# Layer 0's experts computed with units on partitions; layer 1 ranks keys in three pieces per tile; three copies moved to ScalarE; new order tables for both layers

## The reference

```python
x = L0_attn_x                                  # (8, 512, 256)
xn = layernorm(x)
x = x + gated_retention(xn) + experts(xn)      # layer 0
xn = layernorm(x)
x = x + state_space(xn) + mixed_attention(xn)  # layer 1

# experts: E=8, hidden 128, the two best of eight per token
scale = softmax(xf @ gate_w), zero but for each token's top 2
xs = scale.T[:, :, None] * xf[None]            # the INPUT is scaled, per expert
h  = silu(xs @ w1) * (xs @ w3)
out = (h @ w2).sum over experts
```

## Time and profile before

| | us |
|---|---|
| median of 3 runs | 2124.76 |
| lowest, highest | 2121.08, 2131.89 |
| the profiled execution | 2114.17 |
| its span, first to last instruction | 2112.4 |

### The profile page before, as it was taken

One profiled execution on the slowest core, in us unless ns is written; L12 is line 12 of the kernel. 1 busy time (PEld: TensorE's weight loads), 2 busy tenths in 40 slices (PEclk: granted clock), 3 DMA queues, 4 the chain that ended last, 5 costly groups with the idle time before them and its releaser, 6 DMA issues.

```text
span 2112.4 us, 44569 instructions
## 1 busy us (share of the span) xinstructions
PE 1967.1 (93%) x14499; PEld 1188.0 (56%) x14499; DVE 1676.8 (79%) x3065; ACT 1287.0 (61%) x2889; POOL 1396.8 (66%) x1053
## 2 busy tenths in 40 slices
PE   7999999999999977698999999999999998998898
PEld 4666666666666654454464564554554554654555
DVE  5777677677776743598888988989988989989997
ACT  4453534444353425468669779679678678678664
POOL 3433333435233320598888989989979979979996
PEclk9999999999999998699999999999999999999999
DMA  5111202021111116423534533633633533643621
GB/s 150 38 47 49 64 21 62 26 62 44 43 39 34 44 53 188 121 70 111 159 91 112 163 103 97 163 108 92 168 105 108 160 109 93 170 122 90 166 85 31
DMA packets 117427, 198.84 MB, mean 94 GB/s; under 512 B 27688, under 2 KB 64456, under 8 KB 117200
## 3 DMA queue, kind: packets, MB, share of 16 engines
q1 hardware_dynamic: 117200, 196.00, 33.6%
HBM read 148.94 MB, written 46.99 MB: 93 GB/s over the span
## 4 chain that ended last, share of the span: by engine, by line
PE 36%; POOL 11%; issue 7%; DVE 7%; ACT 1%; POOLq 0%; DMA 0%; DVEq 0%; SPq 0%; ACTq 0%
PE bank L1776 32%; POOL HB L1721 7%; POOL HB L1727 4%; PE bank L1876 2%; DVE HB L2244 2%; DVE Sel L2232 1%; DVE bank L2244 1%; PE bank L1782 1%; POOL SD L1747 1%; PE bank L1796 1%; DVE Sel L2230 1%; DVE nmax L2268 0%; DVE HB L2249 0%; PE bank L1848 0%; POOL G L1731 0%
## 5 line engine op out<-in xcount | busy, mean ns | idle before, releaser
L1721 POOL TENSOR_TENSOR HB<-DD,BC 128x512 f32<-128x512 f32 x512 | 643.9, 1284 | 92.3 <-PE bank L1776 73.4
L2058 ACT ACTIVATE bank<-DD,A 128x512 f32<-128x512 f32 x512 | 349.4, 690 | 102.4 <-DVE HB L2249 74.9
L1727 POOL TENSOR_TENSOR HB<-HB,BC 128x512 f32<-128x512 f32 x256 | 331.0, 1304 | 40.9 <-DVE HB L2244 40.6
L2244 DVE TENSOR_TENSOR_SCAN bank<-bank,HB 128x512 f32<-128x512 f32 x256 | 312.0, 1219 | 33.8 <-POOL HB L1721 17.2
L2244 DVE TENSOR_TENSOR_SCAN HB<-bank,HB 128x512 f32<-128x512 f32 x256 | 310.6, 1213 | 13.6 <-ACT bank L2058 6.1
L444 POOL TENSOR_TENSOR hr<-hs,half 128x16 f32<-128x16 f32 x32 | 93.0, 2907 | 250.9 <-DVE hs L968 250.9
L469 PE MATMUL bank<-W,XT 128*128 128x512 f32 x512 | 242.7, 621 | 4.1 <-DVE KT L896 4.0
L2249 DVE TENSOR_TENSOR HB<-bank,BC 128x512 f32<-128x512 f32 x256 | 175.3, 685 | 13.4
L469 PEld LDWEIGHTS bank<-W,XT 128*128 128x128 f32 x512 | 98.9, 200 | 117.5 <-issue 116.3
L1776 PE MATMUL bank<-HB,fold 128*32 128x512 f32 x1024 | 137.2, 607 | 19.5 <-POOL HB L1727 12.3
L1999 ACT ACTIVATE PT<-bank 128x512 f32<-128x512 f32 x192 | 113.0, 594 | 61.4 <-PE bank L1876 61.2
(11 more groups left out here) (236 smaller groups left out, 4069.8 us busy)
## 6 DMA issues: line engine op xcount, KB each, us to landing
DD<-dd_scratch SPq DMA_DIRECT2D x512, 128.0 KB, 3.4
ROW<-row_scratch SPq DMA_DIRECT2D x64, 256.0 KB, 4.0
BC<-ssm_scratch SPq DMA_DIRECT2D x128, 128.0 KB, 4.7
US<-us_scratch SPq DMA_DIRECT2D x32, 512.0 KB, 4.5
us_scratch<-U SPq DMA_DIRECT2D x8, 1024.0 KB, 4.2
us_scratch<-SD SPq DMA_DIRECT2D x8, 1024.0 KB, 6.5
dd_scratch<-SD SPq DMA_DIRECT2D x8, 1024.0 KB, 4.2
dd_scratch<-U SPq DMA_DIRECT2D x8, 1024.0 KB, 6.5
```

Of the source, the lines that this page charges most:

```text
L1721: done(pool.tensor_tensor(HB[:, c % HR], du, bc, ALU.mult), "dbu")
L1727: done(pool.tensor_tensor(h, h, bc, ALU.mult), "cg")
L2058: done(act.activation(PD[n % 2][:], delta, ACT.Exp, scale=A[:, k:k + 1]), "dA")
L2244: done(dve.tensor_tensor_scan(h if n % 2 else dA, dA, h, 0.0, ALU.mult, ALU.add), "scan")
```

## The change

1. Layer 0's experts are turned: hidden units stand on partitions. The scales are transposed (`ct`, PE), copied to SBUF (`ctc`, ACT), stored to DRAM (`cst`, SP) and read back as a row that is broadcast to all partitions, one expert at a time (`cld`, SP, 3 buffers). POOL multiplies XT by that row (`xs`, 128x1024, 2 buffers). `up` has an expert's W1 or W3 as the stationary operand and streams XS, 512 tokens. SiLU and the product are one instruction each per expert (128x512), written to HT, which is already the operand that `dn` needs: `ht` and `htc` go. `wo` and all eight experts of a tile are summed in one PSUM bank, so that one `ya` per tile remains.
2. `dec`, `SQ`, `junk`, `prod` shrink to two buffers or fewer (SBUF space).
3. `rank` compares the keys of earlier tiles with >=, those of its own and later tiles with >, and tests ties in its own 128 only. `ranks` is two additions.
4. `xtv`, `stv` and the copy of the two heavy `widenc` (now `widenr`) go from DVE to ACT.
5. All the order tables have new numbers.

```diff
-L0_PERIOD = 260.34
+L0_PERIOD = 296.85
+                def scales_store(b):
+                    after(sp, "ctc", b, 0)
+                    if b >= 2:
+                        scales_read(sp, b - 2, E - 1)
+                    sp.dma_start(scr["sc"][b % 2].rearrange("(q p) -> q p", p=P), CT[0:NT * E]) \
+                      .then_inc(over["sc_st"], 16)
+
+                def scales_load(b, e):
+                    sp.wait_ge(over["sc_st"], 16 * (b + 1))
+                    n = E * b + e
+                    if n >= SCS:
+                        after(sp, "xs", *divmod(n - SCS, E))
+                    row = scr["sc"][b % 2, e * T:(e + 1) * T].unsqueeze(0).broadcast_to([P, T])
+                    sp.dma_start(SCB[:, n % SCS], row).then_inc(over[f"sc_in{n % SCS}"], 16)
+                def scaled_input(b, e):
+                    after(pool, "xta", b, 0)
+                    after(pool, "xtv", b, 0)
+                    row = scales_loaded(pool, b, e)
+                    after(pool, "up", *lag(b, e, 2, E))
+                    done(pool.tensor_tensor(XS[:, e % 2], XT[:, b % 2], mid(row, ND), ALU.mult), "xs")
+                def turn_scales(b):
+                    after(pe, "ew2", b, 0)
+                    bank = claimed(pe, "ct", b, 0)
+                    done(pe.transpose(bank[0:NT * E, 0:P], SC[:, b % 2].rearrange("p e t -> p (e t)"), ident[:]), "ct")
-                            q = mm(bank[:], xt[:, k, t * P:(t + 1) * P],
-                                   W[:, k, 4 * g:4 * g + 4].rearrange("p e h -> p (e h)"), k == 0, k == ND - 1)
+                            q = mm(bank[:], W[:, k, e], XS[:, e % 2, k], k == 0, k == ND - 1)
-                def turn_hidden(b, n):
...
+                def down(b, t):
+                    after(pe, "ogc", b, t)
+                    after(pe, "hd", b, *range(E))
...
+                    for k in range(ND):
+                        mm(bank[:, 0:D], OGT[:, k, rows], Wo[:, k], k == 0, False)
+                    for e in range(E):
+                        q = mm(bank[:, 0:D], HT[:, e, rows], W2[:, e], False, e == E - 1)
+                def hidden_silu(b, e):
+                    after(act, "up", b, e)
+                    after(act, "dn", b - 1, *range(NT))
+                    done(act.activation(HT[:, e], banks.of["up", b, 2 * e][:], ACT.Silu), "si")
+                def hidden(b, e):
+                    after(dve, "si", b, e)
+                    done(dve.tensor_tensor(HT[:, e], banks.of["up", b, 2 * e + 1][:], HT[:, e], ALU.mult), "hd")
...
-                    own(dve.tensor_scalar(KJ[:, 0], KR[:], KC[:, t:t + 1], None, ALU.is_gt, ALU.add,
-                                          accum_out=ahead[:, t:t + 1]))
-                    own(dve.scalar_tensor_tensor(out=KJ[:, 1], in0=KR[:], scalar=KC[:, t:t + 1],
-                                                 in1=before[:, (3 - t) * P:(3 - t) * P + T],
-                                                 op0=ALU.is_equal, op1=ALU.mult, accum_out=ties[:, t:t + 1]))
+                    own_tile = slice(t * P, (t + 1) * P)
+                    if t:
+                        own(dve.tensor_scalar(KJ[:, 0, 0:t * P], KR[:, 0:t * P], KC[:, t:t + 1], None, ALU.is_ge, ALU.add,
+                                              accum_out=ahead[:, 0, t:t + 1]))
+                    own(dve.tensor_scalar(KJ[:, 0, t * P:], KR[:, t * P:], KC[:, t:t + 1], None, ALU.is_gt, ALU.add,
+                                          accum_out=ahead[:, 1, t:t + 1]))
+                    own(dve.scalar_tensor_tensor(out=KJ[:, 1, 0:P], in0=KR[:, own_tile], scalar=KC[:, t:t + 1],
+                                                 in1=before[:], op0=ALU.is_equal, op1=ALU.mult,
+                                                 accum_out=ties[:, t:t + 1]))
```

More of the change, by code:

```diff
@@ new lines @@
+    "x_ld": [-875.81],
+    "bn": [-763.34, -789.48, -798.06, -824.33],
+    "agg": [-747.25],
+    "rs1": [-731.67],
+    "xn1": [-645.44, -668.0, -632.76, -682.52],
+    "xt": [-549.41, -546.41],
+    "xta": [-538.03],
+    "xtv": [-539.83],
+    "sm": [-528.01],
+    "smc": [-510.44],
+    "ga": [-500.78],
+    "gl": [-486.97],
+    "gm": [-497.17],
+    "gx": [-453.82],
+    "ew0": [-402.53],
+    "ew1": [-353.32],
+    "ew2": [-292.61],
+    "ct": [-278.03],
+    "ctc": [-277.28],
+    "cst": [-242.4],
@@ L297, in lag, with scales_read, scales_loaded @@
             return (b, t - n) if t >= n else (b - 1, t + count - n)
[L299 to L304, removed]
+        def scales_read(eng, b, e):
+            n = E * b + e
+            for m in range(max(n - SCS + 1, 0), n + 1):
+                eng.wait_ge(over[f"sc_in{m % SCS}"], 16 * (m // SCS + 1))
+        def scales_loaded(eng, b, e):
+            n = E * b + e
+            eng.wait_ge(over[f"sc_in{n % SCS}"], 16 * (n // SCS + 1))
+            return SCB[:, n % SCS]
         with nc.Block() as block:
@@ L793, in _ @@
                         hidden_silu(b, i)
[L794 to L795 removed]
+                    elif what == "ctc":
+                        scales_turned(b)
             @block.vector
@@ new lines @@
+    "ssm": [-86.102],
+    "ssmc": [-85.841],
+    "ssm_st": [-84.459],
+    "dt_ld": [-78.255],
+    "abs": [-61.875, -57.944, -74.582, -68.648],
+    "sexp": [-54.145],
+    "relu": [-70.772, -61.822, -36.311, -40.936],
+    "sln": [-49.381],
+    "del": [-43.372, -30.319],
+    "du": [-40.007, -30.297],
+    "dd_st": [-23.626],
+    "xrt": [-65.423, -59.553],
+    "xrtc": [-64.131, -55.098],
+    "k_ld": [-62.642],
+    "rank": [-29.71, -14.81, -6.725, -23.568],
+    "ranks": [3.121],
+    "sel": [13.514, 20.757, 17.944, 20.82],
@@ L2117, in _ @@
                         copied(XT[:, 0], "xt", b, 0, "xta")
+                    elif what == "xtv":
+                        after(act, "del", b - 1, 0)
+                        copied(XT[:, 1], "xt", b, 1, "xtv")
                     elif what == "xr":
@@ L2152, in _ @@
                         copied(SelT[:, 0], "st", b, 0, "sta")
+                    elif what == "stv":
+                        after(act, "tail", b - 1, *range(NT))
+                        copied(SelT[:, 1], "st", b, 1, "stv")
+                    elif what == "widenr":
+                        after(act, "widen", b, NT + i)
+                        after(act, "tail", b - 1, *range(NT))
+                        done(act.activation(YR[:, i], PB[6 + i % 2][:, 0:D], ACT.Copy), "widenr")
                     elif what == "turnc":
@@ L2306, in _ @@
                 number()
+                own(dve.memset(ahead[:, 0, 0:1], 0.0))
                 for what, b, i in plan:
@@ L2317, in _ @@
                         bound(b)
-                    elif what == "xtv":
-                        turned(b)
                     elif what == "conv":
@@ L2339, in _ @@
                         widened(b, i)
-                    elif what == "stv":
-                        selected(b)
                     elif what == "tailc":
```

764 lines of the change are left out of this document (349 added, 415 removed), and 175 rows, old and new, of tables (AT, FIRST, L0_AT, LAST).

## The result

The changed kernel takes 2066.7 us (median of 4 timed runs, 2061.9 to 2072.7) beside 2128.3 us (2121.1 to 2135.8) for the kernel before on the same chip: ratio 0.971, 95% interval 0.967 to 0.976, that is 51 to 71 us faster. The profiled execution took 2064.1 us, 50.1 less than that of before.

A forecast was written before the change was run, and what follows sets the result against it. PE was taken to bound layer 0, and PE, DVE and POOL in turns layer 1. Layer 0's -20 and layer 1's -14 make -34 us, from the timed 2124.8 to 2091 us; range 2056 to 2122.

The forecast's parts named there:

- PE bounds layer 0: Layer 0: PE, busy 669.5 of 679.0 us, sets the time, so work taken off it comes off the time.
- Transposes -28: Layer 0, PE: the 64 `ht` that go, at 0.44 us each, save 28 us.
- The lock's +4: Layer 0: DVE waits for POOL's `xs` at the shared SBUF ports; 4 us reach PE, bounds 0 to 27.
- The head's +3: Start of layer 0: `up` comes later, behind scales, transpose, DRAM round trip and `xs`; 3 us lost, bounds 0 to 8.
- Layer 0 together: Sum for layer 0: -28 + 1 + 4 + 3 = -20 us, bounds -30 to +10.
- The carried 10.6 us: Whole kernel: the old profiled execution, 2114.2 us, was 10.6 below the timed median, 2124.8; this difference was carried over.
- Layer 1: Layer 1: -2 us per period from DVE's relief and the new order, bounds -6 and +5; about -14 us over seven periods.
- The ranking: Layer 1, DVE: shorter tie tests against more comparisons and a second `ranks` addition, net -0.2 us per batch.
- A period 5 us shorter: Rival, layer 1: the new tables also shorten the period by 5 us, giving 2058 us; chance 0.22.
- Layer 1 gives nothing: Rival: PE and POOL keep their load in layer 1, so only layer 0's -20 remains, 2105 us; chance 0.13.
- The lock eats layer 0: Rival: DVE's state chain waits for `xs`, PE's idle time grows by 20; layer 0 at 0, 2119 us; chance 0.10.
- What was to show it: Signs: layer 0 ending near 759 us, batch 91.5, period 151 to 153, XS 2.3 to 2.8, line 974 over 0.9.

The follow-up runs named there:

- e5: Changed kernel with 32 transposes per batch put into layer 0, results overwritten; ratio 0.983 to the kernel before, 25 us slower than the changed kernel.
- e10: Changed kernel with each of layer 0's 64 `hd` on DVE done twice; ratio 0.977 to the kernel before.
- e2: Layer 0 of the kernel before joined to layer 1 of the changed kernel; ratio 0.994 to the kernel before, 6 to 19 us less.
- e9: Changed kernel with POOL's `xs` in layer 0 done twice for every second expert; ratio 1.001 to the kernel before, 64 us slower than the changed kernel.
- e6: Kernel before with 24 of 32 transposes per batch left out of layer 0; ratio 0.993 to the kernel before, 15 us faster.
- e8: Changed kernel with each `z` projection in layer 1 made with one of its two matmuls; ratio 0.970 to the kernel before.
- e11: Changed kernel with each POOL `gate` in layer 1 made on 64 of its 512 columns; ratio 0.974 to the kernel before.
- e3: Kernel before with layer 1's new work (copies on ACT, ranking in three pieces) in the old order; ratio 0.996, 9 us less than before.

## Why the prediction was right, and where its size was off

- **PE bounds layer 0.** Right: putting the transposes back cost 24 to 25 us, nearly the 28 forecast, and PE stayed at 99%.
- **Transposes -28.** In all four traces of the old kind they take 3.7 us per batch by the distances between starts, 29.7 in all; `e5` gives 24 to 25, in an execution whose other matmuls were quick.
- **The lock's +4.** Its size was wrong by 8. DVE's longer instructions came: L1019 by 0.6 us, the state chain's L974 by 0.22. A batch went from 94.7 to 88.6 us, and DVE's busy time in it from 67.5 (456.26 x 94.7 / 640) to 65.3; 54 us less in eight batches would be 6.8 less per batch, and it is 2.2, so that 4.6 us per batch or 37 us are delay, near the 40 forecast. But nothing of it reached PE: its idle time between 100 and 740 fell by 4.3 us. The step that failed is the one that let every saved eviction count only as "earlier", in a bracket of the lower bound. The additions to X had been PE's largest waits, 6.7 of its 9.5 idle us, and with 32 in place of 96 these waits are gone. No run puts the additions back; but in `e10`, with DVE's load given back by other work, PE has no wait for X either.
- **The head's +3.** Not seen: PE waits 3.48 us at 50.21 for v in place of 3.10 for KT at 41.45.
- **Layer 0 together.** -20 forecast, -33 between the two profiled executions, -36 between the means of four and five traces. By the distances between starts, in all traces of the two kinds: transposes -29.7, `dn` 115.6 to 116.4 us before and 111.9 now, -4, waits -4, `ct` +1.5, together -36. The 4 us of `dn`, the same 512 records in rows of 16, had no term in the sum. The carried 10.6 us hid more: the old kernel's profiled execution was below all of its timed runs, the new one's 2.6 below its median, which makes -50 in the profiles -58 in the medians. The carry itself was no firm number: the same old kernel had medians of 2117, 2122, 2126 and 2128 us in the four groups of runs here.
- **Layer 1.** -14 forecast, -19 by the traces and 6 to 19 by the times. The period was to be 151 to 153; it is 152.7 to 153.7 in the new kernel's trace and 153.3 in the mean of six, where it was 154.9. Five of them give 8 us. The other 11 lie in the first batch and at the end, which the counting of quarters did not look at. The ranking stayed as it was, as forecast (-0.2): 4 x (0.54 + 1.31) + 3 x 0.46 + 11 x 0.08 + 0.22 + 1.20 = 11.1 us per batch, before, with its eight read-outs of 0.08 us, 4 x (0.73 + 1.70) + 8 x 0.08 + 0.83 = 11.2. The ties' 1.31 us is what was forecast.
- **The rivals.** A period 5 us shorter: no, it is 1.6 shorter. PE's unchanged sum is a likely reason, since even 3.5 us less of PE gives only 1.8, but that isn't shown. The measured 2067 lies nearer to this rival's 2058 than to the forecast, for other reasons than the rival's: layer 0 and the carry gave what the forecast lacked. Layer 1 gives nothing: refuted by `e2`, though the shortest periods moved by only half a microsecond or so, from 153.8 to between 152.7 and 153.7. The lock eats layer 0: refuted. But `e9` shows how near a loss was: mostly through one `xs` 2.4 us later and the clock that went with the waits, less through the lock.
- **What was to show it.** POOL 59% (58 forecast), PE 99% (98), XS 2.38 us: right; DVE 74% (70 to 73): a little over. The batch at 88.6 (91.5) and the end at 745.6 (759): too high. Line 974's mean over 0.9 us: wrong, 0.81; it was the product in front of it (0.42 to 0.78 us) and L1019 behind it that grew.

The Trainium skill's rule of the exclusive lock ("SBUF — State Buffer", "🔬 SBUF: two separate sides") agrees with the two products above, 1.58 and 2.45 us beside POOL in place of 0.42: each has two inputs in SBUF and ends, at 217.58 and 220.07, 0.28 us after the GpSimd instruction that was running when it began. What it costs the kernel stood in no such row, only in PE's waits.

## What to carry to other kernels

Where an engine bounds a stretch, price each removed instruction of its neighbours by the wait that it was releasing, not by its busy time: the bound engine's list of waits names them, and here it named X. Before work is put on an engine with room, find what may not start until it is done and how late that is; here the share of 59% did not tell it, the distance of 3 us did. When an instruction is long beside another engine, look whether it was as long in the faster kernel before it is blamed. And when one trace of a kernel is the anchor, read the granted clock of its stretch first, since equal code differed by 14 and 17 us, most of it in step with the clock.

## What the runs showed that was not expected

- The granted clock went down where PE waited more: over 100 to 740 us it was 0.95 to 0.98 in all runs with up to 17 us of PE idle, and 0.93 and 0.94 in the two with 26 and 29. In `e9` that is 19 to 32 us, as much as the waits themselves. Up to 17 us there is no such order: `e6`, with 17, had 0.98, `e8` and `e11`, with 5, 0.96. That the waits are the cause was not tried apart.
- The second addition of `ranks`, four columns wide, takes 1190 ns in the median and 164 at the least, beside a POOL that is 90% busy. In `e11`, with 4 us per batch less of POOL, six of its eight take 0.16 to 0.31 us, and in `e3`, with all of POOL's work but the old order, seven of its eight take 0.16. So the place in the order seems to decide it, and not POOL's share alone.
